# Turning the attention's probabilities one step later, with two buffers and a new order of every engine's calls

## The reference

```python
# layer 1: a small network that is trained while it runs, one step per sequence
def step(params, x):                       # params = W1, b1, W2, b2; hidden size 32
    z = x @ t_k.T ; y = x @ t_v.T
    grads = jax.grad(loss_fn)(params, z, y)          # mean of (z + gelu(z W1' + b1) W2' + b2 - y)^2
    new_params = p - LR * g
    out = _recon(new_params, x @ t_q.T)
    return new_params, out
x = x + scan(step, (W1, b1, W2, b2), layernorm(x))

# layer 2: attention with a window and a sink, then a choice of 4 of 32 experts
h = rmsnorm(layernorm(x)); q, k, v = h @ qkv_w + qkv_b       # 16 heads of 64, 4 key heads
q, k = rope(q), rope(k)
logits = q k' / 8, masked to i - 128 <= j <= i
attn = exp(logits - logaddexp(logsumexp(logits), sink))
x1 = layernorm(x) + attn v @ proj_w + proj_b
h2 = rmsnorm(x1); topv, topi = top_k(h2 @ gate_w + gate_b, 4); gw = softmax(topv)
y2 = sum over the chosen experts of gw * (silu(g) * u) @ W_down     # u, g = h2 @ W_up
x = x + x1 + y2
```

## Time and profile before

| | us |
|---|---|
| median of 3 runs | 1218.06 |
| lowest and highest | 1217.37, 1222.43 |
| profiled execution | 1224.69 |
| its span, first to last instruction | 1222.9 |

### The profile page before, as it was taken

The page is one execution under the profiler, slowest core; times in us unless marked ns, Lnnn a source line. Parts: engine busy times, 40 slices in busy tenths (PEclk is TensorE's granted clock), DMA queues, the critical chain, the costliest instruction groups (busy, mean ns, idle before and its releaser), DMA issues. The chain is left out here.

```text
span 1222.9 us, 21965 instructions
## 1 busy us (share of the span) xinstructions
PE 951.9 (78%) x6783; PEld 702.7 (57%) x6865; DVE 778.4 (64%) x2648; ACT 608.3 (50%) x1987; POOL 495.6 (41%) x643
## 2 busy tenths in 40 slices
PE   4778888897989888898988988888877399777710
PEld 2445666565666666575666666555555288666610
DVE  4455687778677776868786777877764344333307
ACT  1017565655646565655756555665654155444400
POOL 2221223334334333334343333434432457777760
PEclk7788999899889899998989989998997599999855
DMA  5999999990000000000000000000000144443119
GB/s 142 267 356 376 374 376 371 370 300 10 16 6 18 9 15 11 11 10 11 15 8 18 6 15 11 11 15 11 15 15 15 55 115 134 132 115 104 52 54 338
DMA packets 98372, 131.54 MB, mean 108 GB/s; under 512 B 15025, under 2 KB 54866, under 8 KB 98258
## 3 DMA queue, kind: packets, MB, share of 16 engines
q1 hardware_dynamic: 84690, 108.36, 26.9%
q0 software_dynamic: 9216, 19.68, 4.6%
q10 hardware_dynamic: 4352, 2.10, 0.6%
HBM read 30.34 MB, written 99.75 MB: 106 GB/s over the span
## 5 line engine op out<-in xcount | busy, mean ns | idle before, releaser
L1152 POOL TENSOR_TENSOR l_t_cos<-l_t_cos,l_t_sin 128x512 f32<-128x512 f32 (+1 forms) x96 | 104.4, 1088 | 434.1 <-DVE l_t_sin L830 434.1
L1020 ACT ACTIVATE l_prob<-l_score,l_nm 128x128 f32<-128x128 f32 (+1 forms) x512 | 210.8, 431 | 0.0
L393 PE MATMUL l_turned<-ident_sb,l_prob 128*128 128x128 f32 x768 | 127.3, 291 | 90.2 <-DVE l_prob L678 52.4
L1345 POOL DMA_INDIRECT expert_out<-e_yo,e_dest x160 | 153.7, 960 | 69.1 <-issue 37.2
L1030 ACT COPY l_probT<-l_turned 128x512 f32<-128x512 f32 x192 | 113.0, 589 | 102.5 <-PE l_turned L393 101.5
L393 PEld LDWEIGHTS l_turned<-ident_sb,l_prob 128*128 128x128 f32 x768 | 91.4, 149 | 108.2 <-issue 107.3
L94 POOL DMA_INDIRECT expert_rows<-h,slot x128 | 128.9, 1007 | 37.6 <-issue 32.4
L694 DVE TENSOR_REDUCE l_mx<-l_score 128x2 f32<-128x512 f32 (+1 forms) x192 | 122.7, 680 | 10.6 <-PE l_score L379 10.2
L555 PE MATMUL l_side_q<-wqkv_sb,l_hT 128*128 128x512 f32 x186 | 118.5, 725 | 12.0 <-issue 4.1
L379 PE MATMUL l_score<-l_kT,l_qT 64*128 64x128 f32 (+1 forms) x1024 | 115.4, 356 | 0.0
L1020 ACT ACTIVATION_READ_ACCUMULATOR l_prob<-l_score,l_nm 128x1 f32 x512 | 110.7, 216 | 0.0
(11 more groups left out here) (234 smaller groups left out, 1937.2 us busy)
## 6 DMA issues: line engine op xcount, KB each, us to landing
expert_rows<-zeros SPq DMA_DIRECT2D x32, 2240.0 KB, 21.9
e_xt<-expert_rows SPq DMA_DIRECT2D x160, 70.0 KB
e_rows<-expert_out SPq DMA_DIRECT2D x16, 512.0 KB, 5.9
wup_sb<-in_wup SPq DMA_DIRECT2D x1, 4096.0 KB, 14.5
expert_out<-e_yo,e_dest POOLq DMA_INDIRECT x160
expert_rows<-zeros SPq DMA_DIRECT2D x32, 70.0 KB, 2.1
expert_rows<-zeros SPq DMA_DIRECT2D x4, 560.0 KB, 12.9
expert_rows<-h,slot POOLq DMA_INDIRECT x128, 2.3
```

The costliest lines, as they stand in the source:

```text
L393: ins = tr(turned[h][:, k * P:(k + 1) * P], prob[:, h, k * P:(k + 1) * P], ident[:])
L1020: ins = A_.activation(prob[:, h, cols], score[(2 * u + h) % 3][:, cols], ACT.Exp, bias=nm[:, b, h, j:j + 1], scale=0.125, accum_out=sums[: ...
L1152: g.tensor_tensor(t_cos[:, c % 2, 0:w], t_cos[:, c % 2, 0:w], t_sin[:, c % 2, 0:w], ALU.add).then_inc(s["added"], 1)
L1345: g_.indirect_dma_start(m["ys"], bass.IndirectOffsetOnAxis(ap=dest[:, g % FOUND, j:j + 1], axis=0), yo[:, g % YO, j, :], None).then_inc(se ...
```

## The change

- `prob`, `sums` and `rec` get two buffers, taken in turn by the unit's number, and `vv` (values) three. `exps` wait for the turn of the unit two before.
- `quotients` becomes three calls: `sums_out` and `recips` work on both halves of a unit at once, `scaled` on one half. `maxima` becomes `maxima`, `shifts` and `sinks`.
- A unit's turn and values come about one slot later, so those of the last units fall into the next iteration. `run` begins one iteration earlier and ends one later for that.
- The loop over slots and the table `side` are gone: each engine's `iteration` is a written list of calls.

```diff
-        vv = sb("vv", [P, 2, TPS, KV * DH])
+        vv = sb("vv", [P, 3, TPS, KV * DH])
-        sums, rec = (sb(n, [P, 2, 4]) for n in "sums rec".split())
-        prob, probT = sb("prob", [P, 2, 512]), sb("probT", [P, 2, 512])
+        sums, rec = (sb(n, [P, 2, 2, 4]) for n in "sums rec".split())
+        prob, probT = sb("prob", [P, 2, 2, 512]), sb("probT", [P, 2, 512])
...
-            for n in range(SEQS + 4):
+            for n in range(-early, SEQS + 4 + late):
```

TensorE's list (`chunk` issues `qkv`, `idle` issues `keep_clock` in the iterations that had it):

```diff
+                project(n, par, 1, 0)
+                qk_turn(n - 1, 1 - par, 5)
+                norm_turn(n - 1, 1 - par)
+                values(n - 1, 1 - par, 4)
+                idle(n, par, 0)
+                turn_probs(n - 1, 1 - par, 5, 0)
+                x_turn(n, par)
+                chunk(n, par, 0)
...
+                a_products(n, par)
+                chunk(n, par, 1)
+                values(n - 1, 1 - par, 5)
+                turn_probs(n, par, 0, 0)
+                scores(n, par, 2)
+                turn_probs(n, par, 0, 1)
+                z_rows(n, par)
+                qk_turn(n, par, 1)
+                project(n, par, 0, 0)
+                project(n, par, 0, 1)
+                chunk(n, par, 2)
+                values(n, par, 0)
+                turn_probs(n, par, 1, 0)
+                scores(n, par, 3)
+                idle(n, par, 4)
+                turn_probs(n, par, 1, 1)
+                residual_cols(n, par)
+                idle(n, par, 5)
+                qk_turn(n, par, 2)
...
+                scores(n, par, 5)
+                turn_probs(n, par, 3, 0)
+                turn_probs(n, par, 3, 1)
+                output(n, par)
+                idle(n, par, 10)
+                qk_turn(n, par, 4)
+                values(n, par, 3)
+                ranks(n, par)
+                idle(n, par, 11)
+                chunk(n, par, 5)
+                turn_probs(n, par, 4, 0)
+                scores(n + 1, 1 - par, 0)
+                gradients(n, par)
+                turn_probs(n, par, 4, 1)
```

VectorE's sums and its list:

```diff
-                one = 2 * done - 1 + h
-                v.wait_ge(s["es_out"], done)
-                v.wait_ge(s["exped"], one)
-                V.tensor_tensor(sums[:, h, 0:w], sums[:, h, 0:w], es[:, b, h, 0:w], ALU.add).then_inc(s["den"], 1)
+                v.wait_ge(s["es_out"], done)
+                v.wait_ge(s["exped"], 2 * done)
+                V.tensor_tensor(sums[:, b, :, 0:w], sums[:, b, :, 0:w], es[:, b, :, 0:w], ALU.add).then_inc(s["den"], 1)
...
+                sinks(n, par, 1)
+                first_stats(n, par, 3)
+                rope(n, par, 1)
+                first_stats(n, par, 4)
+                a_bias(n, par)
+                slots(n - 1, 1 - par)
+                maxima(n, par, 2)
...
+                scaled(n, par, 1, 0)
+                attended(n, par)
+                scaled(n, par, 1, 1)
+                rope(n, par, 2)
...
+                sums_out(n, par, 4)
+                maxima(n, par, 5)
+                recips(n, par, 4)
+                shifts(n, par, 5)
+                one_hot(n, par)
+                output(n, par)
+                scaled(n, par, 4, 0)
+                scaled(n, par, 4, 1)
+                rope(n, par, 5)
+                sinks(n, par, 5)
+                places(n, par)
+                maxima(n + 1, 1 - par, 0)
+                first_stats(n, par, 10)
+                shifts(n + 1, 1 - par, 0)
+                update(n, par)
+                normed_rows(n, par)
+                sinks(n + 1, 1 - par, 0)
+                x_norm(n + 1, 1 - par)
+                sums_out(n, par, 5)
```

ScalarE's `exps`, and GpSimd's list:

```diff
-                after(act, s["t_ps"], 2 * done - 3 + h)
+                after(act, s["t_ps"], 2 * done - 5 + h)
...
+                rope_add(n, par, 1)
+                send(n, par, 0)
+                send(n, par, 1)
+                rms2(n, par)
+                rope_add(n, par, 2)
+                rope_add(n, par, 3)
+                send(n, par, 2)
+                rope_add(n, par, 4)
+                norms(n, par)
+                rope_add(n, par, 5)
+                last_sends(n, par)
+                send(n, par, 3)
+                rope_add(n + 1, 1 - par, 0)
+                spread(n, par)
```

More of the change, by code:

```diff
@@ L656, in _ @@
             pe.wait_ge(s["ready"], 3)
-            run(iteration)
+            run(iteration, 1, 1)
         @block.vector
@@ L1242, in _ @@
             input_scales(2, 6, TILES)
-            run(iteration)
+            run(iteration, 1, 0)
 def experts(m):
```

301 lines of the change are left out of this document (195 added, 106 removed).

## The result

The changed kernel takes 1045.87 us (median of 4 runs, 1044.72 to 1046.67) against 1219.35 (4 runs, 1217.37 to 1222.43): a ratio of 0.8575, 95% interval 0.8553 to 0.8596. The profiled execution took 1046.03, with a span of 1044.3.

The account below looks back on a forecast made before the run. No engine is full; TensorE's waits, mainly for scaled probabilities, and half clock cost time. Iterations 98 + iteration before 6 + drain 14 - ramp 4 - late turns 2 = 112 off 1218: 1106 us; own range 1078 to 1135, 8 in 10 1078 to 1160.

Parts of the forecast that it names:

- the fourth wait: TensorE's long wait at the turn of the normed rows behind the weight update, 1.58 us; forecast to go.
- the rivals: Three cases against the forecast: VectorE becomes the bound (1150 us, chance 0.18), the second rival and the third rival.
- the third rival: Sends queued on GpSimd ahead of the attention's output get longer and hold TensorE up: slower, 1235 us at 3.9 us; chance 0.06.
- the second rival: TensorE waits as long for ScalarE's copies, GpSimd or VectorE's order instead: little or no gain, 1212 us; chance 0.06.
- the iteration, 46.5 us: Forecast length of each of twelve full iterations, 44.4 + 2.1, between 45.0 and 48; 98 us saved over all twelve.
- I take 2.1 in all: TensorE's waits left per iteration: thin places 0 to 2.2 plus small waits 0.5 to 1.0, taken in the upper part.
- unit 4's turn: Thin place at unit 4's turn and the ranks: VectorE 5.0 to 6.1 us against TensorE's 5.0, wait 0 to 1.1.
- the seam: Thin place between two iterations: VectorE 3.6 us and 0.2 for handovers against TensorE's 3.5, wait 0 to 0.3.
- third rotated chunk: Thin place at that chunk's turn: GpSimd and VectorE 5.0 to 5.9 us against TensorE's 5.7, wait 0 to 0.8.
- The floor of 44.4: TensorE's iteration without waits and at full clock: 54.6 - 6.6 - 1.0 - 2.6 = 44.4 us.
- the half clock: TensorE's slow-clock loss in a steady iteration: at most 3.3 us, taken as 2.6; most of it was to go.
- The drain: Stretch after the twelve full iterations, 135.5 us with 28 idle on TensorE: half saved, 14 us (0 to 21).

Follow-up runs that it names:

- the 1192 us run: Kernel before the change with two probability buffers, turn and values one step later (third values buffer), old order, sums per half: 1191.94 us, ratio 0.9757.
- The filled waits: Kernel before the change with 24 throwaway products per full iteration put where TensorE waits: 1196.68 us, ratio 0.9788.

## Why the prediction fell short

**Right.** The mechanism and its signs: the long waits in front of the transposes and of the normed rows' turn are gone, the clock is full (1.00 granted over the twelve iterations), TensorE is the bound, the fourth wait went, iteration 0 is longer (from 26.9 to 30.8 us between the turns of the input, with the loaded input 1.35 later at VectorE in this trace, at 23.76 instead of 22.41), the expert phase did not move. Of the rivals none came: VectorE has 8.4 us free an iteration, a send takes 0.98 us in the median where it took 0.97 (at most 1.36 and 1.24; the longest of any run is 1.53, the third rival's were 3.6 and 3.9), no wait took a new name. In the 1192 us run the second rival did come, in its words ("the wait only changes its name"): the changed kernel, with all written lists, doesn't show it.

**The step that failed is the iteration, 46.5 us, measured 43.46**: 12 times 3.0 are 36 of the 67 us that are missing between 112 and 178.6.
- *"I take 2.1 in all" for remaining waits*: none is there, 25 of the 36 us. The laying out took the old lists' durations, and these contain collisions that the new lists avoid. At unit 4's turn, given "0 to 1.1", the one-hot with its picks was put at 2.2 or 1.1 us; it takes 1.11 (470.22 to 471.33), and there is no wait. Put back beside GpSimd's add the two take 2.20 (427.79 to 429.99) and TensorE waits 0.83. So the place and both its bounds were seen rightly; to take the upper part of the range was wrong. At the seam the normed rows, put at 1.52, take 0.70. There and at the third rotated chunk the trace shows no wait either; these were not tried apart.
- *The floor of 44.4*: 43.5. Idle time was 54.60 - 46.69 = 7.91, not the 7.6 counted, and TensorE's busy time fell by 3.19, where the half clock was put at 2.6. No run shows the 2.6: it is the author's estimate, under the 3.3 that a clock of 0.94 leaves of 54.6 us. The filled waits, which add work and leave waits, shortened the iteration by 2.3. The 0.9 are 11 us. Of the two half-rate stretches, with 0.50 of the full clock granted, one begins at 453.4, behind its wait; the other begins at 470.5, within the wait that ends at 471.00 and not behind it.

**The drain**, "half, since chains of one sequence run there": 14, less 2 for late turns; measured 34.2, by marks that begin 5.5 us earlier and end 17.6 later. Two terms failed. In the forecast's own stretch (803.0 to 938.5) the transposes' waits for VectorE were 19.8 of the 28 idle us, and nearly all of them went: from the mark of iteration 15 to the first send TensorE's idle time fell from 35.3 to 11.8 us. And the clock, though 0.90 there in the earlier trace rows, got no term: over the same stretch it rose from 0.88 to 0.96, and TensorE's busy time fell by 10.7 us (123.3 to 112.6). Together 22 us are missing.

**Iteration 3**, 6 saved: 9.7, since it too has TensorE almost full (idle 8.3 before, 1.3 after) and its busy time fell by 2.7. **The ramp**, 4 lost: 0.5 won. Iteration 0 lost its 3.9, and 4.4 came back up to the mark of iteration 2, where the forecast named "up to 4.4 back" and counted on next to none. In four traces with this ramp iteration 0 takes 29.1 to 30.8 us and that mark lies at 88.8 to 91.2, so the 3.9 is near the upper end of what the order costs there, and the 0.5 is not told from nothing; a loss of 4 would be. How much came back by the statistics done early and how much by the new order stays open: with the bias alone in its old place nothing changed.

The range's own working is off: the terms' bounds, all taken at once, give 1074 to 1147, not 1078 to 1135. The measured time lies outside either.

**VectorE's 2.3 us less** an iteration: 6.1 (41.22 to 35.09). The merged sums, to which the forecast gave all of it, are 0.4 in the new list. The one-hot, the normed rows, the squares and the second norm's rows, each before and after:

```profile
L890 DVE TENSOR_TENSOR l_hot<-iota_e,l_idxf 128x128 f32<-128x128 f32 x32 | 23.2, 764 | 0.5
L968 DVE TENSOR_TENSOR l_hot<-iota_e,l_idxf 128x128 f32<-128x128 f32 x32 | 7.9, 288 | 0.5
...
L795 DVE TENSOR_SCALAR l_hn<-x_all,l_mv,l_rms 128x128 f32<-128x128 f32 x32 | 23.5, 775 | 17.2 <-POOL l_rms L1174 17.2
L873 DVE TENSOR_SCALAR l_hn<-x_all,l_mv,l_rms 128x128 f32<-128x128 f32 x32 | 11.3, 393 | 1.3 <-POOL l_rms L1337 1.3
...
L853 DVE CUSTOM_DVE_ANT_0 l_x2sq<-l_x 128x128 f32<-128x128 f32 x32 | 19.9, 656 | 0.6
L931 DVE CUSTOM_DVE_ANT_0 l_x2sq<-l_x 128x128 f32<-128x128 f32 x32 | 8.0, 289 | 0.6
...
L864 DVE TENSOR_SCALAR h<-l_x,l_ss 128x128 f32<-128x128 f32 x32 | 13.9, 474 | 3.1 <-POOL l_ss L1184 3.1
L942 DVE TENSOR_SCALAR h<-l_x,l_ss 128x128 f32<-128x128 f32 x32 | 8.0, 292 | 3.0 <-POOL l_ss L1347 3.0
```

That is 45 us over the run, or 2.8 an iteration, of collisions with GpSimd: in the trace before, 57 instructions of these groups take over 0.5 us, and every one of them overlaps an elementwise operation of GpSimd; in the trace after there are 2. Sums and reciprocals fell by 2.2 us an iteration and scalings by 0.8; since splitting the sums again costs only 0.4, most of that comes with their new places. That they no longer stand one behind the other is the likely reason, not tested. Not every operation is slowed by an add beside it: the one-hots take 1.59 us beside it (427.79 in the run that moves them back) and 0.49 without it (470.22 in the changed kernel); the maxima take 1.29 with it beside them (468.62 in the changed kernel) and 1.28 without (430.06 in the run that moves the one-hot back). Why the ones are slowed and the others not, no run shows.

## What to carry to other kernels

When an order is forecast by laying durations along it, ask of each duration what ran beside it in the old order; otherwise the waits of the old order are counted into the new one. A hand-written order of several in-order queues is one object: a second buffer or one exchanged list is worth nothing or less here, while moving one or two calls pays if it puts what other engines wait for ahead of what nobody does, and pays next to nothing where a second wait stands behind the first, just as long. Where the bottleneck engine's granted clock falls to half, as it did here at some of TensorE's waits, count the half-rate stretches beside the waits: here TensorE's busy time fell by 3.2 us beside 7.9 us of idle time in an iteration, and by 10.7 beside 23.5 in the drain.

## What the runs showed of the hardware

- Products that nobody reads, issued into TensorE's waits, kept the granted clock at 1.00 where it had been 0.94 and took 2.1% (1.7 to 2.5) off the time, although 57 us of waits for VectorE were left at those places.
- In the changed kernel the clock is granted in full (1.00) from 97.2 to 766 us without a break; before, it fell to 0.50 at least once in each of the twelve full iterations. In the one of the earlier trace rows it fell twice, to 0.50 from 453.4 to 456.8, behind the wait of 1.41 us, and from 470.5 to 473.9, within and behind that of 1.58, and not at the waits of 1.98 and 1.60, where it stayed at 1.00.
